# The first attention of a two-layer kernel rewritten: keys spread only within a pair of heads, scores of two pairs in different array rows, value products in groups of four, the layer norm chain on GpSimd

## What the reference computes

```python
x = x + tanh(g_xattn[0]) * L0_attention(layernorm(x), ctx)   # sigmoid of the scores, 16 heads of 16
x = x + tanh(g_ffn[0])   * L0_experts(layernorm(x))          # best of 8 experts, 256->1024->512->256
x = x + tanh(g_xattn[1]) * L1_attention(layernorm(x), ctx)   # softmax, mask, biases
x = x + tanh(g_ffn[1])   * L1_ffn(layernorm(x))              # best of 2 experts, plus a shared one
```

```python
q = (layernorm(x) @ Wq.T) * 16 ** -0.5;  k = ctx @ Wk.T;  v = ctx @ Wv.T    # per head: 16 columns
o = sigmoid(q @ k.T) @ v                                                    # 512 x 64 scores per batch and head
x = x + tanh(g) * (o @ Wo.T)
```

## Time and profile before

| | |
|---|---|
| median of 3 runs | 932.6 us |
| lowest, highest | 932.09, 935.45 us |
| span of the profiled execution, first to last instruction | 914.7 us |
| time of that execution itself | not listed; the median less the span is 17.9 us, which lie around the instructions |
| instructions | 14862 |
| busy: PE, PEld, DVE, ACT, POOL | 724.8, 634.7, 534.9, 338.7, 173.1 us |
| mean granted TensorE clock | 0.882 of full |

### The profile page before, as it was taken

One profiled execution on the slowest core, in us unless ns is written; L12 is line 12 of the kernel. 1 busy time (PEld: TensorE's weight loads), 2 busy tenths in 40 slices (PEclk: granted clock), 3 DMA queues, 4 the chain that ended last, 5 costly groups with the idle time before them and its releaser, 6 DMA issues. The chain is left out here.

```text
span 914.7 us, 14862 instructions
## 1 busy us (share of the span) xinstructions
PE 724.8 (79%) x4920; PEld 634.7 (69%) x4921; DVE 534.9 (58%) x1357; ACT 338.7 (37%) x586; POOL 173.1 (19%) x209
## 2 busy tenths in 40 slices
PE   3799992077899998999935476886648799999998
PEld 3445542076899988999834354665447799999997
DVE  4565334155775467644627888795446655665556
ACT  5434331144543245422525235434224233333322
POOL 1000000700000000000023285454026000112500
PEclk9699995578999999999976677888757999999999
DMA  8910000724540015500013000000036101111202
GB/s 299 416 56 1 1 0 9 299 81 145 180 152 23 23 69 189 189 23 23 23 33 99 23 24 0 1 1 1 1 100 211 65 24 47 46 46 40 86 0 92
DMA packets 20931, 71.79 MB, mean 78 GB/s; under 512 B 4098, under 2 KB 8451, under 8 KB 16803
## 3 DMA queue, kind: packets, MB, share of 16 engines
q1 hardware_dynamic: 13730, 49.76, 15.2%
q0 software_dynamic: 7168, 21.63, 8.0%
HBM read 44.65 MB, written 26.74 MB: 78 GB/s over the span
## 5 line engine op out<-in xcount | busy, mean ns | idle before, releaser
L1023 ACT ACTIVATE e_h<-psum,e_be 128x256 f32<-128x256 f32 x144 | 67.6, 474 | 154.0 <-PE psum L50 149.2
L48 PE MATMUL psum<-e_h_hi,e_w_hi 128*128 128x256 f32 x384 | 110.2, 287 | 5.4 <-DVE e_w_lo L1090 4.7
L1295 ACT ACTIVATE f_h<-psum,f_b 128x256 f32<-128x256 f32 x136 | 63.8, 473 | 125.6 <-PE psum L50 119.3
L49 PE MATMUL psum<-e_h_lo,e_w_hi 128*128 128x256 f32 x384 | 107.9, 281 | 0.0
L50 PE MATMUL psum<-e_h_hi,e_w_lo 128*128 128x256 f32 x384 | 107.8, 281 | 0.0
L1082 DVE CAST e_h_hi<-e_h 128x256 fp32r<-128x256 f32 x144 | 43.4, 301 | 92.7 <-ACT e_h L1023 90.4
L48 PE MATMUL psum<-f_w_hi,f_h_hi 128*128 128x256 f32 x272 | 78.2, 288 | 2.4 <-DVE f_h_lo L1348 2.3
L48 PEld LDWEIGHTS psum<-e_h_hi,e_w_hi 128*128 128x128 f32 x384 | 72.3, 188 | 8.9 <-DVE e_w_lo L1090 8.1
L50 PE MATMUL psum<-f_w_hi,f_h_lo 128*128 128x256 f32 x272 | 76.8, 282 | 0.0
L49 PE MATMUL psum<-f_w_lo,f_h_hi 128*128 128x256 f32 x272 | 76.8, 282 | 0.0
L49 PEld LDWEIGHTS psum<-e_h_lo,e_w_hi 128*128 128x128 f32 x384 | 72.4, 188 | 0.0
(11 more groups left out here) (288 smaller groups left out, 1968.8 us busy)
## 6 DMA issues: line engine op xcount, KB each, us to landing
e_w_raw<-in_W SPq DMA_DIRECT2D x18, 1024.0 KB, 5.7
xs<-zeros SPq DMA_DIRECT2D x6, 1024.0 KB, 8.9
ys<-zeros SPq DMA_DIRECT2D x6, 1024.0 KB, 13.5
w_raw<-in_fw SPq DMA_DIRECT2D x12, 512.0 KB, 4.6
ys<-e_yo POOLq DMA_DIRECT2D x14, 256.0 KB, 2.8
e_xg<-xs POOLq DMA_DIRECT2D x13, 256.0 KB, 3.2
e_w_raw<-in_W SPq DMA_DIRECT2D x6, 512.0 KB, 7.9
ys<-x_norm POOLq DMA_DIRECT2D x10, 256.0 KB, 2.5
```

The costliest lines, as they stand in the source:

```text
L48: nc.tensor.matmul(out, wh, xh, start=start, stop=False)
L49: nc.tensor.matmul(out, wh, xl, start=False, stop=False)
L1023: nc.scalar.activation(h32[:, m % 2], ps[:, 2 + m % 2, 0:SLOT], ACT.Gelu, bias=be[:, m:m + 1]).then_inc(gelu_ok, 1)
L1295: nc.scalar.activation(h32[:, m % 2], ps[:, 2 + m % 2, 0:SLOT], ACT.Relu, bias=b1[:, f * MH + m:f * MH + m + 1]).then_inc(relu_ok, 1)
```

## The change

Only the first attention changes; `attention_phase` stays for L = 1. It does this:

- The keys: `kz_hi` and `kz_lo` have, for each pair, the pair's own 32 rows only, with the two heads apart (even and odd, by the column `odd`). ACT and DVE write them with 2 instructions each in place of 16.
- The scores: `scores(b, g)` makes two pairs at once. A matmul takes 32 rows (those of its pair) in place of 128; the two pairs of a group stand in different rows of the array, take turns in the program, and write banks 4 and 5. One sigmoid takes both banks (128x1024). Before the next group is written, its sigmoid must be over (`p_ok`).
- The values: `weighted(b, c)` makes four value products directly behind each other, into four partition ranges of one bank, twice per batch.
- The layer norm: DVE keeps bn_stats, bn_aggr, the added epsilon and the seed of the inverse square root (one instruction in place of two). The chain after it (`normalise`, 15 operations of 128x4 in place of 11, each waiting for the one before) runs on GpSimd, for all eight statistics (`NORMS`) in order.
- The high part of the output moves from DVE to ACT (`output_hi`).
- The order: the transposes of batch 1 stand before the loop, `input_T(s + 2)` in step s, and the rest is arranged anew as shown. The first layer norm stands ahead of the low parts of the weights on DVE.

What the left out part holds is as before: `input_T`, `q_proj`, `rows_T`, `logits`, `project`, `residual` and SP's transfers, with the waits that the new order needs. Set-up waits on each batch of x by itself.

```diff
--- before.py
+++ after.py
...
+def normalise(nc, pool, mv, half, tmp, rstd, shift, step, count):
+
+    def link(ins):
+        nonlocal count
+        count += 1
+        ins.then_inc(step, 1)
+        pool.wait_ge(step, count)
+
+    link(nc.gpsimd.tensor_scalar(half, mv[:, :, 1], EPS, -0.5, ALU.add, ALU.mult))
+    for _ in range(3):
+        link(nc.gpsimd.tensor_tensor(tmp, rstd, rstd, ALU.mult))
+        link(nc.gpsimd.tensor_tensor(tmp, tmp, half, ALU.mult))
+        link(nc.gpsimd.tensor_scalar(tmp, tmp, 1.5, None, ALU.add))
+        link(nc.gpsimd.tensor_tensor(rstd, tmp, rstd, ALU.mult))
+    link(nc.gpsimd.tensor_tensor(shift, mv[:, :, 0], rstd, ALU.mult))
+    return nc.gpsimd.tensor_scalar(shift, shift, -1.0, None, ALU.mult), count
+
+
+def sigmoid_attention(nc, k, io):
+
+    GROUPS = PAIRS // 2
+
+    NORMS = [(0, 0), (1, 0), (2, 0), (0, 1), (3, 0), (1, 1), (2, 1), (3, 1)]
+    NTH = {n: i for i, n in enumerate(NORMS)}
...
+        kz_hi, kz_lo = (sb(n, [P, C, B, 2, KEYS], F32R) for n in ("kz_hi", "kz_lo"))
+        odd = sb("odd", [P, 2])
+        prob = sb("prob", [P, GROUPS, 2, S])
...
+            steps = 0
+            for q in range(len(NORMS)):
+                pool.wait_ge(mv_ok, q + 1)
+                last, steps = normalise(nc, pool, ln_mv[:, q], ln_half[:], ln_tmp[:],
+                                        ln_rstd[:, q], ln_shift[:, q], ln_step, steps)
+                last.then_inc(rs_ok, 1)
+                pool.wait_ge(rs_ok, q + 1)
+
+        @block.scalar
+        def _(act):
+            def norm(b, kind, out, done):
+                q = NTH[b, kind]
+                act.wait_ge(rs_ok, q + 1)
+                for i in range(TB):
+                    last = nc.scalar.activation(out[:, i, :], k["x"][:, b * TB + i, :], ACT.Identity,
+                                                bias=ln_shift[:, q, i:i + 1], scale=ln_rstd[:, q, i:i + 1])
+                last.then_inc(done, 1)
+
...
+            def sigmoid(b, g):
+                n = b * GROUPS + g
+                act.wait_ge(s_done, n + 1)
+                if b:
+                    act.wait_ge(pv_done, C * (b - 1) + g // 2 + 1)
+                nc.scalar.activation(prob[:, g], ps[:, 4:6, :], ACT.Sigmoid, scale=SCALE).then_inc(p_ok, 1)
+
+            def output_hi(b, c):
+                if b and c == 0:
+                    act.wait_ge(y_done, TB * b)
+                act.wait_ge(pv_done, C * b + c + 1)
+                nc.scalar.activation(oT_hi[:, c], ps[:, 6 + c, :], ACT.Copy).then_inc(oh_ok, 1)
...
+            for w in range(4):
+                nc.scalar.activation(w_hi[:, w], w_raw[:, w], ACT.Copy).then_inc(wh_ok, 1)
+            norm_1(0)
+            act.wait_ge(kp_done, 1)
+            nc.scalar.activation(kT[:].rearrange("p c b n -> p c (b n)"), ps[:, 4:6, 0:B * KEYS], ACT.Copy).then_inc(kT_ok, 1)
+            act.wait_ge(odd_ok, 1)
+            act.wait_ge(kT_ok, 1)
+            for a in range(2):
+                nc.scalar.activation(kz_hi[:].rearrange("p c b a n -> p (c b) a n")[:, :, a, :],
+                                     kT[:].rearrange("p c b n -> p (c b) n"), ACT.Copy,
+                                     scale=odd[:, a:a + 1]).then_inc(kzh_ok, 1)
+            input_hi(0)
+            q_hi(0)
+            norm_1(1)
+            input_hi(1)
+            act.wait_ge(g_ld, 16)
+            nc.scalar.activation(k["tg"][:], k["g_raw"][:], ACT.Tanh).then_inc(tg_ok, 1)
+
+            for s in range(B + 1):
+                if s < B:
+                    sigmoid(s, 0)
+                if s >= 1:
+                    norm_2(s - 1)
+                if s + 1 < B:
+                    q_hi(s + 1)
+                if s < B:
+                    sigmoid(s, 1)
+                if s >= 1:
+                    act.wait_ge(t2_done, s)
+                    if s > 1:
+                        act.wait_ge(lg_done, s - 1)
+                    nc.scalar.activation(xrT[:], ps[:, 0:2, :], ACT.Copy).then_inc(th2_ok, 1)
+                if s < B:
+                    sigmoid(s, 2)
+                    output_hi(s, 0)
+                if s + 2 < B:
+                    norm_1(s + 2)
+                if s < B:
+                    sigmoid(s, 3)
+                    output_hi(s, 1)
+                if s + 2 < B:
+                    input_hi(s + 2)
+
+        @block.vector
+        def _(dve):
+            def statistics(b, kind):
+                q = NTH[b, kind]
+                for i in range(TB):
+                    last = nc.vector.bn_stats(ln_st[:, i, :], k["x"][:, b * TB + i, :])
+                last.then_inc(bn_ok, 1)
+                dve.wait_ge(bn_ok, 3 * q + 1)
+                for i in range(TB):
+                    last = nc.vector.bn_aggr(ln_mv[:, q, i, :], ln_st[:, i, :])
+                last.then_inc(bn_ok, 1)
+                dve.wait_ge(bn_ok, 3 * q + 2)
+                nc.vector.tensor_scalar(ln_var[:], ln_mv[:, q, :, 1], EPS, None, ALU.add).then_inc(bn_ok, 1)
+                dve.wait_ge(bn_ok, 3 * q + 3)
+                nc.vector.tensor_scalar(ln_rstd[:, q].bitcast(I32), ln_var[:].bitcast(I32), -0.5, float(RSQRT_SEED),
+                                        ALU.mult, ALU.add).then_inc(mv_ok, 1)
+                dve.wait_ge(mv_ok, q + 1)
+
...
+            dve.wait_ge(mk_ok, 2)
+            nc.vector.tensor_reduce(odd[:], k["head_rows"][:].rearrange("p (j a) -> p a j", a=2), AX.X, ALU.add).then_inc(odd_ok, 1)
...
+            norm_1(0)
+            for w in range(4):
+                weights_lo(w)
...
+            for s in range(B + 1):
+                if s >= 1:
+                    statistics(s - 1, 1)
+                if s + 2 < B:
+                    norm_1(s + 2)
+                if s + 1 < B:
+                    q_lo(s + 1)
+                if s < B:
+                    output_lo(s, 0)
+                if s >= 1:
+                    logits(s - 1)
+                if s < B:
+                    output_lo(s, 1)
+                if s + 2 < B:
+                    input_lo(s + 2)
+                if s < B:
+                    residual(s)
+
+        @block.tensor
+        def _(pe):
...
+            def scores(b, g):
+                n = b * GROUPS + g
+                if n:
+                    pe.wait_ge(p_ok, n)
+                c, first = divmod(2 * g, PAIRS // C)
+                q_hi, q_lo = qT_hi[:, b % 2, c], qT_lo[:, b % 2, c]
+                pairs = [(ps[:, 4 + j, :], slice(2 * HD * (first + j), 2 * HD * (first + j + 1))) for j in range(2)]
+                for out, r in pairs:
+                    nc.tensor.matmul(out, kz_hi[r, c, b].rearrange("p a n -> p (a n)"), q_hi[r], start=True, stop=False)
+                for out, r in pairs:
+                    nc.tensor.matmul(out, kz_hi[r, c, b].rearrange("p a n -> p (a n)"), q_lo[r], start=False, stop=False)
+                for out, r in pairs:
+                    last = nc.tensor.matmul(out, kz_lo[r, c, b].rearrange("p a n -> p (a n)"), q_hi[r], start=False, stop=True)
+                last.then_inc(s_done, 1)
+
+            def weighted(b, c):
+                pe.wait_ge(p_ok, b * GROUPS + 2 * c + 2)
+                if b:
+                    pe.wait_ge(ol_ok, C * (b - 1) + c + 1)
+                for j in range(PAIRS // C):
+                    last = nc.tensor.matmul(ps[2 * HD * j:2 * HD * (j + 1), 6 + c, :], vz[:, b, c * PAIRS // C + j, :],
+                                            prob[:, 2 * c + j // 2, j % 2, :], start=True, stop=True)
+                last.then_inc(pv_done, 1)
...
+            input_T(0)
+            q_proj(0)
+            input_T(1)
+            pe.wait_ge(c_ld, 32)
+            pe.wait_ge(kzl_ok, 2)
+            pe.wait_ge(vz_ok, B)
+            pe.wait_ge(ql_ok, 1)
+            scores(0, 0)
+            for s in range(B + 1):
+                if s + 1 < B:
+                    q_proj(s + 1)
+                if s < B:
+                    scores(s, 1)
+                if s >= 1:
+                    rows_T(s - 1)
+                if s < B:
+                    scores(s, 2)
+                    weighted(s, 0)
+                    scores(s, 3)
+                if s >= 1:
+                    logits(s - 1)
+                if s < B:
+                    weighted(s, 1)
+                if s + 1 < B:
+                    pe.wait_ge(ql_ok, s + 2)
+                    scores(s + 1, 0)
+                if s + 2 < B:
+                    input_T(s + 2)
+                if s < B:
+
+                    if s >= 1:
+                        pe.wait_ge(lg_ok, s)
+                    project(s)
...
@@ -1515,8 +1962,10 @@
                 if not L:
                     k["zeros"] = isb("zeros", [P, 1024 // P * D])
                 k["xT_hi"], k["xT_lo"] = isb("xT_hi", [P, C, T], F32R), isb("xT_lo", [P, C, T], F32R)
-                attention_phase(nc, k, L, io)
-                if L:
+                if not L:
+                    sigmoid_attention(nc, k, io)
+                else:
+                    attention_phase(nc, k, L, io)
```

218 lines of the change are left out of this document (added).

## The result

The changed kernel takes 946.4 us (median; 945.1 to 948.8) against 932.4 for the kernel before on the same chip: a ratio of 1.014, with a 95% interval of 1.012 to 1.017. It is slower by 1.4%, where 925 us was forecast, 0.8% faster.

The account below looks back on a forecast made before the run. PE would no longer set the pace; each step's dependence on the one before, through GpSimd's chain, would. 58.0 + 25.05 + 2 x 22.95 + 15.6 = 144.5 us against 151.9, so 925 us; range 914 to 938.

Parts of the forecast that it names:

- Value products, four at a time: First attention: two groups of four per batch, 2 x 1.0 us for 7.2, relieving PE of 5.2 us per batch.
- Pairs side by side: Scores in the first attention: 32-row matmuls of two pairs overlap, saving half of 5.5 us, 2.7 us per batch.
- rival (a): Scores: the two pairs do not overlap, a group costs six matmuls, 9.3 us more in all, so 934; chance 0.13.
- The chain on POOL: Layer norm chain moved to GpSimd: 15 links at 0.29 us, C = 4.4 us, against 2.2 on DVE.
- rival (b): GpSimd is the bound: links of 0.49 us, chain 7.35, kernel 943; chance 0.21 with all chains above 5.6.
- The first chain: GpSimd's chain in the start, beside four weight subtractions on DVE: 0.8 us entered for that company on top of 4.4.
- Who waits: In steps 1 to 3, ACT waits for the chain at norm_2 and PE idles some 5 us before rows_T.
- The sum: Whole first attention: 58.0 + 25.05 + 2 x 22.95 + 15.6 = 144.5 us, against 151.9 before.
- a step without another layer norm: Steps 2 and 3, from norm_2 to the batch's residual: N + 16.25, a step of 22.95 us.
- N: When the GpSimd chain ends in a step: 2.3 us plus the chain's 4.4 after the previous batch's residual.
- the start: Up to the end of batch 0's residual: 48.4 us plus two chains plus 0.8 for company, 58.0 us.
- tail: After the last residual, to the last logits: 11.2 us plus one chain, 15.6 us.

Follow-up runs that it names:

- e9: Changed kernel with full-height score tiles and the layer norm chain back on VectorE: attention ends at 145.2 us, ratio 0.9918 to the kernel before.
- e10: e7 plus four useless full-array matmuls in each of two short waits per step and 36 before the last rows_T: attention ends at 123.2 us, ratio 0.9707.
- e11: e8 (full-height scores) plus the same useless matmuls in the waits as e10: attention ends at 132.5 us, ratio 0.9848 to the kernel before.
- e3: Changed kernel plus 20, 20, 36 and 40 useless full-array matmuls before PE's waits for norm_2: attention ends at 148.6 us, ratio 0.9908 to the kernel before.
- e7: Changed kernel with queues reordered to put useful work ahead of each wait, small score tiles kept: attention ends at 140.7 us, ratio 0.9818 to the kernel before.
- e8: e7's queue order with score tiles of full height (128 rows): attention ends at 135.9 us, ratio 0.9842 to the kernel before.
- e4: Changed kernel with a group's six score matmuls written as three of one pair, then three of the other: attention ends at 166.0 us, ratio 1.0158.
- e12: e8 with the layer norm chain on VectorE again: attention ends at 138.1 us, ratio 0.9852 to the kernel before.
- e5: The changed kernel measured again, unaltered, in another batch of runs: attention ends at 165.3 us, ratio 1.0141 to the kernel before.

## Why the prediction was wrong

- **Value products, four at a time: right** as to their price: 1.06 us for four pairs (eight matmul records) at full clock. What they are worth alone no run shows; together with the new order and the rest of the change it is 6.7 us (e9).
- **Pairs side by side: right** as to the overlap (rounds 0.23 apart), and so rival (a) is out. Wrong as to the worth: I counted the half of 5.5 us a batch as a gain; the tiles cost 7.9 us in all, and the clock is lower in each step with them. The gain is there where the clock holds (e10 against e11, 2.7 us in each of steps 2 and 3).
- **The chain on POOL: right.** 0.28 a link, 4.3 us; rival (b), a slow GpSimd, is out, although its time of 943 came nearest. The first chain, with company, took 5.5 us against the 5.2 that I entered. Its links of 0.49 to 0.54 lie beside VectorE's weight subtractions (10.61 to 13.12):

```profile
10.86 0.54 POOL L87 TENSOR_SCALAR a_ln_tmp<-a_ln_tmp 128x4 f32<-128x4 f32 x1
...
12.65 0.53 POOL L86 TENSOR_TENSOR a_ln_tmp<-a_ln_tmp,a_ln_half 128x4 f32<-128x4 f32 x1
13.27 0.22 POOL L87 TENSOR_SCALAR a_ln_tmp<-a_ln_tmp 128x4 f32<-128x4 f32 x1
```

  By the rule that I cited of the Trainium skill's "SBUF — State Buffer" (on the engine ports), each of the two engines holds the other up; the rows agree in kind, at 1.2 us for the chain rather than the 2.7 that was the most by it.
- **Who waits: right.** PE idle for 4.69 and 4.67 us in steps 1 and 2 behind `x_norm` (forecast "some 5"). In step 3 it is 8.42, not 5: there is no further batch to project ahead of the wait. The sum, which counts from the chain's end, isn't touched by it.
- **The failed step: the clock behind the wait, in "a step without another layer norm", from scores 3 on.** I let the clock come back for "scores of group 3, 1.0 (N + 8.3), logits 1.8 (N + 10.0)", values 1.0 and the 3.9 of project and residual. In step 2, N is 99.05. Up to the first values the forecast is met (scores of group 2 end at 104.65, N + 5.6; values at 106.51, N + 7.5). Then scores 3 end 0.7 later than forecast, logits take 1.75 more, values 0.9 more, project and residual 1.6 more: 5.0, all of it the lower clock, and the step is 27.96 for 22.95.
- **The same in the start and the other steps.** The projection of batch 1 begins at 38.59, forecast 38.4. From there to the end of batch 0's residual I forecast 19.6 and it took 24.2, at a clock of 0.61. With misses of 4.75 (start), 4.55, 5.0 and 4.7 (steps) and 0.2 (tail), the 19.2 us between 144.5 and 163.7 are in the main one error made four times; of the start's 4.75, up to 1.5 is within what a start varies by. e3 bears it out: with the same waits and the clock held over them, the attention ends at 148.6, 4 us from the forecast. The sum's structure was sound.
- **Why I made it.** I read in the earlier trace rows that a projection which begins at the lower clock is at full clock after 4.4 us, and carried that to transposes, scores of 32 rows, values and logits. Those rows are of full-array matmuls of 512 columns, and of nothing else. I had priced what the wait does to the clock, but not whether the work behind it would bring the clock back; none of the rivals had that case.
- **The price of the whole.** 19.2 of the 21 us between 925 and 946 are this; 2 are not assigned, and lie within the spread of the runs. The 17.9 us between the span and the median of before, which I took along, do not lie around the instructions, as the table ahead of the prediction says: in the changed kernel's profile only 1.4 us do (943.7 of 945.1). By all appearance they are the longer time behind the attention that some profiles have and that of before lacks (last section), and so in both kernels' medians; no profile of before shows it.

## What to carry to other kernels

Packing small tiles next to each other halves the array's time for them, but count what it does to the clock: where a stage is made of small tiles and short waits, it can run at 1.2 GHz for most of its time, and then costs more than the wide matmuls did (7.9 us here). Look for it in the granted clock of a step, and in the same operation at two durations (1.06 and 1.94 here) with no wait between. The cure was cheap here: put independent work ahead of each wait (e7, e8), and fill what is left with a few full-array matmuls that nobody reads (e10: the attention ends 17 us earlier with 8 of them a step and 36 in the tail; e11, with wide scores: 3.5 us). And when work moves to a slower engine, ask who stands behind it in each queue: the chain on GpSimd cost 12 us in one order and nothing in another.

## What the runs showed of the hardware that I had not expected

- The granted clock falls in the midst of unbroken work that is small tiles and logits (e3, at 104.67), and stays at 1.2 GHz through 17.5 us without an idle stretch, of small tiles, transposes, logits and the first output matmuls (changed kernel, 101.2 to 118.7). The Trainium skill's "TensorE: Matmul & The Clock Gate" (Part 1) makes the clock a matter of how busy the engine has been; here PE is busy for 21.10 of 23.67 us in e7's step 1 at 0.71 and for 19.24 of 21.93 in e8's at 0.92, so the busy time alone doesn't tell it, and the two differ in the height of the score tiles.
- Matmuls in different rows of the array overlap, and did so in e4 too, whose text has the three of one pair ahead of the three of the other.
- What follows the attention takes some 18 us longer in some profiles than in others. In the changed kernel, e10 and e11 it comes with an idle stretch of about 21 us in the last expert phase; in e9 and e12 ACT's waits there come in three pieces, 20.8 us in all with 11.9 the longest, and 12.7 with 5.1. In the changed kernel it is the one below. The trace names no instruction of this core as its cause. It goes with the batch of runs and not with the edit, as the kernel before shows; nor is it the chip: e5 to e8 and e9 to e12 have the same one in their results. Its cause stays open.

```profile
877.68 0.84 ACT L1742 ACTIVATE f_h<-psum,f_b 128x256 f32<-128x256 f32 x2 [21.07 <-remote]
```
